# One order of pieces for the three later batches: rewriting the issue lists of five engines

## The chip, the cores and the metric

The kernel runs on one core of one Trainium2 chip. The metric is the device time of one execution in microseconds (us), less is better. The kernel before took 447.46 us (median of 3 runs, 446.96 to 448.86). One further execution was profiled; it took 444.95 us, and its span from the first to the last instruction is 443.1 us.

## What is computed

The input x holds four batches of 512 tokens with 512 features in fp32. One transformer layer is computed, cut here to what matters:

```
h  = layernorm(x)
q, kv = h @ W_q.T, h @ W_kv.T            # 16 heads of 32
q, kv = fft(q), fft(kv), each divided by its L2 norm over the head
kv = cumsum(kv, over the tokens)
x  = x + real(ifft(q * kv)) @ W_o.T      # the attention half
h  = layernorm(x)
g  = silu((h @ fp8(gate_w)) * gate_scale) * ((h @ fp8(up_w)) * up_scale)
x  = x + (g @ fp8(down_w)) * down_scale  # the feed-forward half, 1536 wide
```

## The kernel before

A batch b is worked in 4 row tiles t of 128 tokens; the feed-forward half runs in 12 steps i of 128 columns, numbered n = 12b + i over all batches. Each of the five engines (PE, ACT, DVE, POOL and the DMA queue SP) runs a list of pieces, strictly in the order in which it is written, and pieces of different engines meet on semaphores. Products that need more than one pass are split in a high part, made by ACT as a copy, and a low part, made by DVE or POOL as a difference.

For one row tile the attention half goes through these pieces. `pe_qk(b,t,w)` (L281): 12 matmuls, q for w=0 and kv for w=1. `act_qk` squares and copies the result, `dve_sum` sums the squares. After all 8 of them come `dve_norm_head`, `act_sqrt1`, `dve_norm_tail` and `dve_scale(b,t,w)` (L893), which divides by the norm. `act_ks` and `pool_ks(b,t)` (L238) make the two parts of the scaled kv. `pe_tri(b,t)` (L294), 2 matmuls, is the running sum over the 128 tokens of the tile. `act_row(b,t)` (L569) then copies the last row and sends it by a small DMA to row 0 of the next tile's position, where `pool_ks(b,t+1)` adds it (L1242) before `act_ks(b,t+1)` and `pool_ks` go on: this is the carry, and it makes the four `pe_tri` of a batch a chain. `dve_product(b,t)` (L899) and `pool_product(b,t)` (L1246, three operations, the last L1257) multiply q with the running sum. `pe_pT` (L307) transposes, `act_pT` and `dve_pT` take the two parts away, `pe_o` (L315) multiplies by W_o with 12 matmuls, and `dve_o` adds to x. After the four tiles come the second layernorm and `pe_hT` (L328), `act_hT`, `dve_hT`.

The feed-forward step n is `pe_gate_up` (L352): 8 matmuls into the one bank bg and 8 into the one bank bu; `act_silu(n)` empties bg, `dve_f(n)` empties bu, `act_fu(n)` and `dve_fu(n)` make the two parts in a buffer with two places, and `pe_down(n)` (L387) adds 8 matmuls to the four banks bd. `act_fu(n)` waits for `pe_down(n-2)`. All attention pieces after batch 0 share the two banks ba, taken in turn by the order that `tenancies()` gives; that order is the same before and after.

Batch 0's attention half, and beside batch 0's feed-forward half the attention half of batch 1, stand in a prologue that is written out piece by piece. It also folds the Fourier matrix into W_q and W_kv (`pe_fold`), into W_o (`pe_wo_high`, `pe_wo_low`), and rounds the gate, up and down weights to fp8 in 18 parts (`sp_weights`, `act_half`, `dve_round`). From then on a loop runs over b = 1, 2, 3: the feed-forward half of b beside the attention half of b + 1, which for b = 3 does not exist. In the kernel before the loop over b holds an inner loop over i with conditions such as `if 5 <= i <= 8: pe_pT(e, nxt, i - 5)`. In it `pe_down(n-1)` follows `pe_gate_up(n)`, with the attention pieces between or behind them.

Of the kernel before, what the change touches and what calls it, by code (L numbers as in the profile page):

```python
# [14 lines left out]
NB = 4  # L15
NT = 4
KT = 4
D = 512
NI = 12
# [63 lines left out]
def build(nc, x, xT, w_q, w_kv, woT, gate_w, up_w, down_w, gs_d, us_d, ds_d, cst_d, cst2_d, out):  # L83
    ctx = ExitStack()
    with ctx:
# [305 lines left out]
        def tensor_program(e):  # L391
# [12 lines left out]
            pe_wo_high(e, 0)  # L404
            pe_wo_high(e, 1)
            pe_wo_high(e, 2)
            pe_wo_low(e, 0)
            pe_pT(e, 0, 0)
            pe_wo_high(e, 3)
            pe_tri(e, 0, 1)  # L410
            pe_wo_low(e, 1)
            pe_wo_low(e, 2)
            pe_wo_low(e, 3)
            pe_tri(e, 0, 2)
            pe_o(e, 0, 0)
            pe_pT(e, 0, 1)
            pe_tri(e, 0, 3)
            pe_pT(e, 0, 2)
            pe_o(e, 0, 1)
            pe_o(e, 0, 2)  # L420
            pe_pT(e, 0, 3)
            pe_qk(e, 1, 0, 0)
            pe_o(e, 0, 3)
            pe_hT(e, 0, 0)
            pe_qk(e, 1, 0, 1)
# [3 lines left out]
            pe_hT(e, 0, 2)  # L429
            pe_hT(e, 0, 3)  # L430
            pe_qk(e, 1, 2, 0)
# [5 lines left out]
            pe_gate_up(e, 0, 2)  # L437
            pe_down(e, 0)
            pe_gate_up(e, 0, 3)
            pe_gate_up(e, 0, 4)  # L440
            pe_down(e, 1)
            pe_tri(e, 1, 0)
            pe_gate_up(e, 0, 5)
            pe_down(e, 2)
            pe_gate_up(e, 0, 6)
            pe_pT(e, 1, 0)
            pe_tri(e, 1, 1)
            pe_down(e, 3)
            pe_o(e, 1, 0)
            pe_gate_up(e, 0, 7)  # L450
            pe_pT(e, 1, 1)
            pe_down(e, 4)
            pe_tri(e, 1, 2)
            pe_down(e, 5)
            pe_o(e, 1, 1)
            pe_gate_up(e, 0, 8)
            pe_down(e, 6)
            pe_pT(e, 1, 2)
            pe_tri(e, 1, 3)
            pe_gate_up(e, 0, 9)  # L460
            pe_down(e, 7)
            pe_o(e, 1, 2)
            pe_pT(e, 1, 3)
            pe_gate_up(e, 0, 10)
            pe_o(e, 1, 3)
            pe_down(e, 8)
            pe_gate_up(e, 0, 11)
            pe_hT(e, 1, 0)
            pe_hT(e, 1, 1)
            pe_down(e, 9)  # L470
            pe_hT(e, 1, 2)
            pe_hT(e, 1, 3)
            pe_down(e, 10)
            for b in range(1, NB):
                for i in range(NI):
                    n, nxt = b * NI + i, b + 1
                    pe_gate_up(e, b, i)
                    if nxt < NB:
                        if i in (0, 1):
                            pe_qk(e, nxt, i, 0)  # L480
                            pe_qk(e, nxt, i, 1)
                        if i == 2:
                            pe_qk(e, nxt, 3, 0)
                            pe_qk(e, nxt, 3, 1)
                        if i == 4:
                            pe_tri(e, nxt, 0)
                        if 6 <= i <= 9:
                            pe_o(e, nxt, i - 6)
                        if 5 <= i <= 8:
                            pe_pT(e, nxt, i - 5)  # L490
                        if i == 10:
                            pe_hT(e, nxt, 0)
                            pe_hT(e, nxt, 1)
                        if i == 11:
                            pe_hT(e, nxt, 3)
                    if 0 < n < NB * NI - 2:
                        pe_down(e, n - 1)
                    if nxt < NB:
                        if i == 1:
                            pe_qk(e, nxt, 2, 0)  # L500
                            pe_qk(e, nxt, 2, 1)
                        if 5 <= i <= 7:
                            pe_tri(e, nxt, i - 4)
                        if i == 10:
                            pe_hT(e, nxt, 2)
# [140 lines left out]
        def scalar_program(e):  # L646

            act_center(e, 0)
            act_minus(e)
            act_center(e, 1)  # L650
            act_center(e, 2)
            act_center(e, 3)
# [3 lines left out]
            act_x(e, 0, 1)  # L656
            act_x(e, 0, 2)
            act_wf(e, 0, 2)
            act_x(e, 0, 3)
            act_wf(e, 0, 3)  # L660
            act_wf(e, 1, 0)
            act_wf(e, 1, 1)
# [5 lines left out]
            act_first_root(e)  # L668
            act_half(e, 2)
            act_qk(e, 0, 0, 1)  # L670
            act_triangle(e)
            act_qk(e, 0, 1, 0)
            act_qk(e, 0, 1, 1)
            act_sqrt1(e, 0, [0, 1])
            act_qk(e, 0, 2, 0)
            act_ks(e, 0, 0)
            act_qk(e, 0, 2, 1)
            act_qk(e, 0, 3, 0)
            act_ks(e, 0, 1)
            act_half(e, 3)  # L680
# [4 lines left out]
            act_x(e, 1, 1)  # L685
            act_wo_low(e, 0)
# [3 lines left out]
            act_ks(e, 0, 2)  # L690
            act_wo_low(e, 1)
            act_wo_low(e, 2)
            act_pT(e, 0, 0)
            act_ks(e, 0, 3)
            act_wo_low(e, 3)
            act_pT(e, 0, 1)
            act_pT(e, 0, 2)
            act_x(e, 1, 2)
            act_half(e, 4)
            act_x(e, 1, 3)  # L700
            act_pT(e, 0, 3)
            act_half(e, 5)
            act_half(e, 6)
            act_sqrt2(e, 0, [0, 1])
            act_hT(e, 0, 0)
            act_qk(e, 1, 0, 0)
            act_sqrt2(e, 0, [2, 3])
            act_hT(e, 0, 1)
            act_qk(e, 1, 0, 1)
            act_qk(e, 1, 1, 0)  # L710
            act_half(e, 7)
            act_hT(e, 0, 2)
            act_qk(e, 1, 1, 1)
            act_hT(e, 0, 3)
            act_qk(e, 1, 2, 0)
            act_qk(e, 1, 2, 1)
# [780 lines left out]
```

## Time and profile before

| | us |
|---|---|
| median of 3 runs | 447.46 (446.96 to 448.86) |
| profiled execution | 444.95 |
| its span | 443.1 |
| PE busy | 425.4, 96% of the span |
| DVE, ACT, POOL busy | 270.6, 186.3, 103.3 |

An engine's busy time is the sum of its instructions' durations in the profile. A row of the timeline gives the start of a run of like instructions, how long it lasts, and in brackets the idle time of the engine ahead of it with what ended it.

### The profile page before, as it was taken

How to read it: one execution, taken by the hardware profiler on the slowest of the kernel's cores; microseconds unless marked ns; L12 is line 12 of the kernel's file. 1: busy time of each engine (PE TensorE's matmuls, PEld its weight loads, DVE VectorE, ACT ScalarE, POOL GpSimd, SP SyncE). 2: the span in 40 equal slices, each digit the busy share in tenths (PEclk: the TensorE clock that was granted, in tenths of full speed). 3: DMA queues.
4: the chain of work that ended last, by engine and by line, in shares of the span. 5: the costliest groups of instructions: out<-in, count | busy, mean ns of one | idle time of the engine just before them, and what ended most of it. 6: DMA issues, size and time to landing. Idle time of an engine off the chain costs nothing.

```text
span 443.1 us, 5468 instructions
## 1 busy us (share of the span) xinstructions
PE 425.4 (96%) x1976; PEld 279.8 (63%) x1976; DVE 270.6 (61%) x488; ACT 186.3 (42%) x299; POOL 103.3 (23%) x107
## 2 busy tenths in 40 slices
PE   4999999999999999999799999999989999999995
PEld 4885678655666666875466657777456665555554
DVE  5999699989687773357655373445836463523224
ACT  4768345665524363236342352345333252222230
POOL 0404820001646002301537110400354100400002
PEclk9999999999999999999999999999999999999999
DMA  8980481011150000700000000320000000200002
GB/s 251 333 324 22 118 278 60 0 29 24 45 191 1 0 2 0 226 12 1 0 0 25 25 2 0 122 69 0 0 2 1 1 0 1 95 1 1 0 1 95
DMA packets 17595, 26.14 MB, mean 59 GB/s; under 512 B 1824, under 2 KB 8224, under 8 KB 17568
## 3 DMA queue, kind: packets, MB, share of 16 engines
q1 hardware_dynamic: 17280, 25.77, 17.5%
q8 instruction: 16, 0.26, 0.2%
q14 instruction: 11, 0.09, 0.1%
q10 hardware_dynamic: 288, 0.02, 0.0%
HBM read 21.57 MB, written 4.19 MB: 58 GB/s over the span
## 4 chain that ended last, share of the span: by engine, by line
PE 86%; POOL 5%; DMA 2%; DVE 2%; ACT 2%; issue 1%; SPq 0%; DVEq 0%; POOLq 0%
PE bd L383 18%; PE bg L367 18%; PE bu L367 18%; PE ba L290 15%; PE ba L324 7%; PE bd L290 3%; POOL qk L1253 2%; PE ba L333 1%; DMA gu<-gate_w_dram 1%; PE ba L303 1%; DMA hT<-w_q_dram 1%; POOL ks L1244 1%; PE ba L312 1%; PE bd L276 1%; POOL qk L1254 1%
## 5 line engine op out<-in xcount | busy, mean ns | idle before, releaser
L383 PE MATMUL bd<-dw,fu 128*128 128x512 f32 x376 | 99.3, 405 | 0.0
L367 PE MATMUL bg<-hT,gu 128*128 128x512 f16 x384 | 91.1, 380 | 0.0
L367 PE MATMUL bu<-hT,gu 128*128 128x512 f16 x384 | 90.7, 379 | 0.0
L383 PEld LDWEIGHTS bd<-dw,fu 128*128 128x128 f32 x376 | 69.6, 188 | 15.7
L972 DVE SCALAR_TENSOR_TENSOR ff<-bu,us,sl 128x512 f32<-128x512 f32 x48 | 35.9, 749 | 62.6 <-PE bu L367 60.8
L290 PE MATMUL ba<-wf,xTs 128*128 128x512 f32 x288 | 69.2, 396 | 0.0
L367 PEld LDWEIGHTS bu<-hT,gu 128*128 128x128 f16 x384 | 37.6, 98 | 45.3
L367 PEld LDWEIGHTS bg<-hT,gu 128*128 128x128 f16 x384 | 34.8, 98 | 45.6 <-issue 8.2
L290 PEld LDWEIGHTS ba<-wf,xTs 128*128 128x128 f32 x288 | 53.7, 188 | 12.0 <-POOL xTs L1236 0.2
L607 ACT ACTIVATE sl<-bg,gs 128x512 f32<-128x512 f32 x48 | 33.0, 688 | 60.8 <-PE bg L367 60.0
L1244 POOL TENSOR_TENSOR ks<-qk,ks 128x512 f16<-128x512 f32 x16 | 19.0, 1185 | 127.1 <-ACT ks L567 127.1
L617 ACT ACTIVATE fu<-ff 128x512 fp32r<-128x512 f32 x47 | 29.5, 629 | 36.2 <-DVE ff L972 33.2
L1262 POOL TENSOR_TENSOR h<-ff,h 128x512 f32<-128x512 f32 x14 | 17.5, 1283 | 114.4 <-DVE ff L994 114.4
L851 DVE TENSOR_REDUCE S<-tu 128x16 f32<-128x512 f32 x32 | 21.7, 682 | 33.4 <-ACT tu L538 33.4
L977 DVE TENSOR_TENSOR fu<-ff,fu 128x512 fp32r<-128x512 f32 x47 | 34.2, 728 | 12.8 <-ACT fu L617 12.8
L324 PE MATMUL ba<-wo,pT 128*128 128x512 f32 x144 | 36.6, 403 | 0.0
L538 ACT ACTIVATE tu<-ba 128x512 f32<-128x512 f32 x24 | 14.3, 597 | 47.4 <-PE ba L290 47.4
L324 PEld LDWEIGHTS ba<-wo,pT 128*128 128x128 f32 x144 | 27.1, 188 | 6.5
L1253 POOL TENSOR_TENSOR qk<-tu 128x256 f32<-128x256 f32 x14 | 16.2, 1160 | 40.2 <-DVE tu L919 40.2
L1236 POOL TENSOR_TENSOR xTs<-xTr,xTs 128x512 fp32r<-128x512 f32 x12 | 15.8, 1322 | 34.4 <-ACT xTs L524 34.4
L567 ACT ACTIVATE ks<-qk 128x512 f16<-128x512 f32 x16 | 10.1, 633 | 30.4 <-POOL qk L1242 23.5
L896 DVE TENSOR_TENSOR qk<-qk,sc 128x512 f32<-128x512 f32 x32 | 21.9, 724 | 0.1
(161 smaller groups left out, 465.3 us busy)
## 6 DMA issues: line engine op xcount, KB each, us to landing
h<-x_dram SPq DMA_DIRECT2D x16, 256.0 KB, 4.1
out_dram<-h SPq DMA_DIRECT2D x16, 256.0 KB, 2.0
xTr<-xT_dram SPq DMA_DIRECT2D x12, 256.0 KB, 4.5
hT<-w_q_dram SPq DMA_DIRECT2D x4, 256.0 KB, 3.2
gu<-w_kv_dram SPq DMA_DIRECT2D x4, 256.0 KB, 5.6
h<-xT_dram SPq DMA_DIRECT2D x4, 256.0 KB, 6.4
hT<-up_w_dram SPq DMA_DIRECT2D x2, 512.0 KB, 4.7
hT<-gate_w_dram SPq DMA_DIRECT2D x2, 512.0 KB, 6.9
```

The lines of the kernel that those rows point to most:

```text
L290: m = e.matmul(ba[i][:, :], xTs[:, part_x, k, P * t:P * t + P], wf[:, w, part_w, k, :], start=k == 0 and part_x == part_w, stop=k == KT - ...
L324: m = e.matmul(ba[i][:, :], src[:, part_p, P * j:P * j + P], wo[:, part_w, j, :], start=j == 0 and part_p == part_w, stop=j == KT - 1 and ...
L367: m = e.matmul(bk[:, :], gu[:, c, 4 * w + k, col:col + P], hT[:, b % 2, part, k, :], start=k == 0 and part == 0, stop=k == KT - 1 and part ...
L383: m = e.matmul(bd[t][:, :], fu_at(n)[:, part, P * t:P * t + P], dw[:, i, :], start=i == 0 and part == 0, stop=i == NI - 1 and part == 1)
L607: e.activation(sl[:, n % 2, :], bg[:, :], ACT.Silu, scale=gs[:, i:i + 1]).then_inc(a_silu, 1)
L617: e.activation(fu_at(n)[:, 0, :], ff[:, n % 2, :], ACT.Copy).then_inc(a_fu, 1)
L851: e.tensor_reduce(S[:, t, NH * w:NH * w + NH], v, AX.X, ALU.add).then_inc(v_sum, 1)
L896: e.tensor_tensor(split_heads(qk[:, t, w, :]), split_heads(qk[:, t, w, :]), head_scale(t, w), ALU.mult).then_inc(v_kn if w else v_qn, 1)
L972: e.scalar_tensor_tensor(out=ff[:, n % 2, :], in0=bu[:, :], scalar=us[:, i:i + 1], in1=sl[:, n % 2, :], op0=ALU.mult, op1=ALU.mult).then_i ...
L977: e.tensor_tensor(fu_at(n)[:, 1, :], ff[:, n % 2, :], fu_at(n)[:, 0, :].bitcast(F32), ALU.subtract).then_inc(v_fu, 1)
L1244: e.tensor_tensor(ks[:, 1, t, :], qk[:, t, 1, :], ks[:, 0, t, :], ALU.subtract).then_inc(p_ks, 1)
L1253: e.tensor_tensor(q_re, t_re, t_im, ALU.subtract).then_inc(p_re, 1)
```

## The change

All five issue lists get a new order; no function that computes, no buffer and no semaphore is changed, and every piece is issued as often as before. The inner loop over i is gone: for each b the pieces stand in one list. PE's list for the loop:

```diff
             for b in range(1, NB):
-                for i in range(NI):
...
-                    pe_gate_up(e, b, i)
...
+                nxt = b + 1
+                if nxt < NB:
+                    pe_qk(e, nxt, 0, 0)
+                    pe_qk(e, nxt, 0, 1)
+                pe_gate_up(e, b, 0)
+                pe_down(e, b * NI - 1)
...
+                pe_gate_up(e, b, 3)
+                pe_down(e, b * NI + 1)
+                pe_gate_up(e, b, 4)
+                pe_down(e, b * NI + 2)
+                if nxt < NB:
+                    pe_tri(e, nxt, 0)
+                pe_gate_up(e, b, 5)
+                pe_down(e, b * NI + 3)
+                pe_gate_up(e, b, 6)
+                if nxt < NB:
+                    pe_pT(e, nxt, 0)
+                    pe_tri(e, nxt, 1)
+                pe_down(e, b * NI + 4)
+                if nxt < NB:
+                    pe_o(e, nxt, 0)
+                pe_gate_up(e, b, 7)
+                if nxt < NB:
+                    pe_pT(e, nxt, 1)
+                pe_down(e, b * NI + 5)
+                if nxt < NB:
+                    pe_tri(e, nxt, 2)
+                    pe_o(e, nxt, 1)
+                pe_gate_up(e, b, 8)
+                if nxt < NB:
+                    pe_pT(e, nxt, 2)
+                pe_gate_up(e, b, 9)
+                if nxt < NB:
+                    pe_tri(e, nxt, 3)
+                    pe_o(e, nxt, 2)
+                pe_down(e, b * NI + 6)
+                if nxt < NB:
+                    pe_pT(e, nxt, 3)
+                pe_down(e, b * NI + 7)
+                if nxt < NB:
+                    pe_o(e, nxt, 3)
+                pe_down(e, b * NI + 8)
+                pe_gate_up(e, b, 10)
+                if nxt < NB:
+                    pe_hT(e, nxt, 0)
+                    pe_hT(e, nxt, 1)
+                pe_gate_up(e, b, 11)
...
```

In POOL's loop `pool_ks(nxt, 0)` and `pool_ks(nxt, 1)` now both stand ahead of `pool_product(nxt, 0)`, where before the product stood between them. In DVE's loop only `dve_scale` of (0,1), (0,0), (1,0), (1,1), (2,0) stand ahead of `dve_product(nxt, 0)`, and behind it `dve_f`, `dve_fu`, `dve_pT(0)` and `dve_product(1)`; before, three `dve_scale` came close behind the first product.

The prologue is reordered as well. The parts that are spoken of below:

```diff
 SP
+            sp_weights(e, 3)
+            sp_weights(e, 8)
             sp_x(e, 0, 2)
+            sp_x(e, 1, 0)
+            sp_weights(e, 11)
+            sp_weights(e, 9)
+            sp_scales(e)
+            sp_wo(e)
...
 ACT
             act_center(e, 2)
+            act_first_root(e)
             act_center(e, 3)
...
 PE
             pe_wo_high(e, 0)
+            pe_tri(e, 0, 1)
+            pe_pT(e, 0, 0)
             pe_wo_high(e, 1)
+            pe_wo_low(e, 0)
...
+            pe_pT(e, 0, 1)
+            pe_o(e, 0, 0)
             pe_tri(e, 0, 2)
             pe_tri(e, 0, 3)
```

Before, `sp_wo` stood ahead of `sp_x(e, 1, 0)`, which waits for `dve_round(2)`; `act_first_root`, the first square root, stood behind `act_half(1)`; and `pe_tri(0, 1)` came behind `pe_wo_high(3)`, `pe_o(0, 0)` behind `pe_tri(0, 2)`.

## Rows read from the trace of the kernel before

**Rows 1.** The page, busy time and the 40 slices of 11.08 us:

```profile
PE 425.4 (96%) x1976; PEld 279.8 (63%) x1976; DVE 270.6 (61%) x488; ACT 186.3 (42%) x299; POOL 103.3 (23%) x107
...
GB/s 251 333 324 22 118 278 60 0 29 24 45 191 1 0 2 0 226 12 1 0 0 25 25 2 0 122 69 0 0 2 1 1 0 1 95 1 1 0 1 95
```

**Rows 2.** Busy time in stretches: attention 0, prologue's rest, b = 1, 2, 3:

```profile
15.32:64.56 49.24, 47.21 (x211) 35.05 (x210) 42.04 (x87) 29.89 (x54) 19.29 (x22) 1.00 0.60 200
64.56:163.51 98.95, 98.89 (x468) 64.55 (x466) 82.84 (x138) 52.48 (x79) 20.68 (x21) 1.00 0.14 46
163.51:268.14 104.63, 102.32 (x473) 66.85 (x473) 56.56 (x103) 41.69 (x68) 30.24 (x29) 1.00 0.10 31
268.14:372.37 104.23, 101.99 (x473) 66.95 (x472) 54.82 (x102) 37.94 (x61) 22.18 (x23) 1.00 0.06 21
372.37:431.90 59.53, 59.53 (x271) 32.86 (x271) 18.75 (x27) 15.22 (x23) 4.98 (x4) 1.00 0.05 19
```

**Rows 3.** PE's waits: us in total, times, longest:

```profile
PE ba L312 <- POOL qk L1257: 3.2, 2, 1.6
PE bd L303 <- POOL ks L1244: 1.3, 1, 1.3
```

**Rows 4.** Timeline of PE in b = 1, steps 4 to 9:

```profile
201.20 1.90 PE L367 MATMUL bg<-hT,gu 128*128 128x512 f16 x8
...
206.50 1.90 PE L367 MATMUL bg<-hT,gu 128*128 128x512 f16 x8
...
209.97 0.59 PE L303 MATMUL ba<-ks,tr 128*128 128x512 f16 x2
...
217.44 0.63 PE L312 MATMUL ba<-cst,qk 128*128 128x128 f32 x4 [1.58 <-POOL qk L1257]
...
220.56 0.59 PE L303 MATMUL ba<-ks,tr 128*128 128x512 f16 x2 [0.65 <-POOL ks L1244]
...
238.69 0.59 PE L303 MATMUL ba<-ks,tr 128*128 128x512 f16 x2
```

**Rows 5.** Timeline of ACT, DVE and POOL in b = 1:

```profile
211.22 0.52 ACTq L575 DMA_DIRECT2D qk<-qk  x1
...
213.16 0.68 DVE L977 TENSOR_TENSOR fu<-ff,fu 128x512 fp32r<-128x512 f32 x1
213.32 2.92 POOL L1253 TENSOR_TENSOR qk<-tu 128x256 f32<-128x256 f32 x1 [4.96 <-DVE tu L919]
213.77 1.88 DVE L896 TENSOR_TENSOR qk<-qk,sc 128x512 f32<-128x512 f32 x3
...
217.24 1.26 POOL L1242 TENSOR_TENSOR qk<-qk 1x512 f32<-1x512 f32 x1
219.25 1.16 POOL L1244 TENSOR_TENSOR ks<-qk,ks 128x512 f16<-128x512 f32 x1 [0.74 <-ACT ks L567]
...
240.75 0.73 POOL L1253 TENSOR_TENSOR qk<-tu 128x256 f32<-128x256 f32 x1 [2.20 <-DVE tu L919]
```

**Rows 6.** DMA issues: KB each, median us from issue to landing:

```profile
gu<-woT_dram SPq DMA_DIRECT2D x1, 1024.0 KB, 10.9
...
qk<-qk ACTq DMA_DIRECT2D x9, 2.0 KB, 1.6
```

**Rows 7.** Timeline of SP and PE in the prologue:

```profile
22.18 0.67 SPq L1367 DMA_DIRECT2D gu<-woT_dram  x1
27.88 0.34 SPq L1332 DMA_DIRECT2D h<-x_dram  x1
...
37.81 1.88 PE L342 MATMUL ba<-gu,sl 128*128 128x512 f32 x4
```

**Rows 8.** Timeline of ACT at the start of the prologue:

```profile
10.06 0.73 ACT L518 ACTIVATE hT<-hT,wmv 128x512 f32<-128x512 f32 x1 [0.43 <-DVE wmv L827]
...
22.34 1.28 ACT L628 ACT_TABLE_LOAD   x1
23.64 0.20 ACT L628 ACTIVATE Q<-Q 128x1 f32<-128x1 f32 x1
```

More of the change, by code:

```diff
@@ new lines, in scalar_program @@
+                act_fu(e, b * NI + 1)
+                if nxt < NB:
+                    act_qk(e, nxt, 3, 0)
+                act_fu(e, b * NI + 2)
+                act_silu(e, b * NI + 3)
+                if nxt < NB:
+                    act_qk(e, nxt, 3, 1)
+                    act_sqrt1(e, nxt, range(NT))
+                act_silu(e, b * NI + 4)
+                if nxt < NB:
+                    act_ks(e, nxt, 0)
+                    act_row(e, nxt, 0)
+                act_fu(e, b * NI + 3)
@@ new lines, in scalar_program @@
+                if b + 2 < NB:
+                    act_x(e, b + 2, 0)
+                act_silu(e, b * NI + 5)
+                if nxt < NB:
+                    act_ks(e, nxt, 1)
+                act_fu(e, b * NI + 4)
+                act_fu(e, b * NI + 5)
+                act_silu(e, b * NI + 6)
+                if nxt < NB:
+                    act_pT(e, nxt, 0)
+                    act_row(e, nxt, 1)
+                act_fu(e, b * NI + 6)
+                if b + 2 < NB:
+                    act_x(e, b + 2, 1)
@@ new lines, in scalar_program @@
+                act_silu(e, b * NI + 7)
+                if nxt < NB:
+                    act_ks(e, nxt, 2)
+                    act_pT(e, nxt, 1)
+                    act_row(e, nxt, 2)
+                act_silu(e, b * NI + 8)
+                if nxt < NB:
+                    act_ks(e, nxt, 3)
+                    act_pT(e, nxt, 2)
+                act_fu(e, b * NI + 7)
+                act_fu(e, b * NI + 8)
+                if nxt < NB:
+                    act_pT(e, nxt, 3)
+                act_silu(e, b * NI + 9)
@@ new lines, in scalar_program @@
+                if nxt < NB:
+                    act_sqrt2(e, nxt, range(NT))
+                act_fu(e, b * NI + 9)
+                if b + 2 < NB:
+                    act_x(e, b + 2, 2)
+                act_silu(e, b * NI + 10)
+                act_fu(e, b * NI + 10)
+                if nxt < NB:
+                    act_hT(e, nxt, 0)
+                    act_hT(e, nxt, 1)
+                act_silu(e, b * NI + 11)
+                if nxt < NB:
+                    act_hT(e, nxt, 2)
+                act_fu(e, b * NI + 11)
@@ new lines, in vector_program @@
+                dve_f(e, b * NI + 3)
+                if nxt < NB:
+                    dve_norm_tail(e, nxt, range(NT))
+                    dve_scale(e, nxt, 0, 1)
+                    dve_scale(e, nxt, 0, 0)
+                dve_f(e, b * NI + 4)
+                if nxt < NB:
+                    dve_scale(e, nxt, 1, 0)
+                    dve_scale(e, nxt, 1, 1)
+                    dve_scale(e, nxt, 2, 0)
+                dve_fu(e, b * NI + 3)
+                if nxt < NB:
+                    dve_product(e, nxt, 0)
```

678 lines of the change are left out of this document (337 added, 341 removed).

## The prediction

> **What bounds the kernel now.** I read the page first. PE is busy for 425.4 of 443.1 us [rows 1], and the change neither adds nor takes away one of its instructions, so all that can be won is time in which PE stands idle: 17.7 us at most. The table of stretches says where that is [rows 2]: subtract PE's busy time from each length. Attention 0 has 2.0 us, the rest of the prologue 0.1, the loop's b = 1 and b = 2 have 2.3 and 2.2, and b = 3 none. The remaining 11 us are the start, ahead of the first projections, and the end, where the last output leaves; the lists order the end as before. The granted clock is 1.00 in every stretch, the upper of TensorE's two levels (2.4 GHz), and PE idles too little anywhere for it to be in question.
>
> Then PE's waits, which name the causes [rows 3]: in total 3.2 us of the first transposes of b = 1 and 2, pT(nxt,0), for the last operation of POOL's product, and 1.3 us in attention 0 for POOL's part of ks. The timeline of b = 1 shows the two gaps of a loop [rows 4]: 1.58 us ahead of pT(2,0) and 0.65 ahead of tri(2,1). b = 2 repeats them within 0.01 us. The other engines' rows tell why [rows 5]: the product of tile 0 started on POOL at 213.32, its first operation took 2.92 us where the same operation at 240.75 took 0.73, while DVE ran operations with two inputs from SBUF beside it (a `dve_fu` at 213.16, three `dve_scale` at 213.77). Only behind it did POOL add the carry (217.24) and make ks of tile 1 (219.25), for which tri(2,1) waited.
>
> **The loop, tile 0.** Prices of pieces on PE: a gate pair is 209.97 - 206.50 = 3.47 us, gate pair and down together 206.50 - 201.20 = 5.30, so a down is 1.83 [rows 4]. Before, one down and one gate pair lay between the tri and the pT of tile 0, and PE came to pT 217.44 - 1.58 - 209.97 = 5.9 us after the tri began, while the product was ready after 7.5. After the change a gate pair, a down and a gate pair lie there, with the tri itself (about 0.4) 9.2 us. What must happen in that time is more than before, since POOL now makes ks of tile 1 first. Counted from the tri's start: the row is sent at 1.25 (211.22) and lands 1.6 later, 2.85 [rows 5, 6]; from the carry's start to ks's start are 219.25 - 217.24 = 2.0, and ks takes 1.16, so 6.0; the product takes 0.73 twice and some 0.3, near 1.8, so 7.8 [rows 5]. One `dve_fu` (0.68) may hold POOL up in it: 8.5. That leaves 0.7 us. With the 2.2 us by which a product was lengthened before (2.92 less 0.73), it would be 10.0 and PE would wait 0.8. But no row of scales is issued beside it now, only f, fu, pT and the next product, so I take 8.5. The tri of tile 1, directly behind this pT, needs ks, which is ready at 6.0 to 6.7. Both gaps go: 2.23 us in each of two loops, -4.5.
>
> **The loop, the other tiles.** Between tri and pT of tiles 1 and 2 lie 8.1 us (down, o, gate pair) and 6.3 (o, gate pair); an o piece is 12 matmuls against a down's 8, so some 2.75. Before, a gate pair and an o lay there and nothing waited. At tile 3 only an o and a down are left, with the tri 5.0 us. In the trace POOL's product starts 240.75 - 238.69 = 2.1 after the tri's start and takes near 1.8, which is 3.9: it fits by 1.1. pT(3) to o(3) is one down and the transpose, 2.2 us, and in it lie ACT's copy and DVE's difference behind the two of fu(8): four operations of 0.63 to 0.7 that overlap pairwise, about 2.0. The three downs 6, 7, 8 stand together; fu(8) waits for the first, then needs 219.25 - (217.24 + 1.26) = 0.75 for a copy and its signal on ACT [rows 5] and 0.68 on DVE, 1.4 against the 1.83 of down(7). These two places are thin, so I add +0.3 for both loops and keep 0 to +1.0. What is behind the waiting `act_fu(8)` on ACT is `act_pT(3)` and `act_silu(9)`, the next gate pair is two downs away, so nothing else is late. For b = 3 the attention pieces are missing, the same fit holds, and its 59.53 us were all busy before: 0.
>
> **The loop's seam.** qk(nxt,0,0) now comes ahead of gate pair 0, directly behind down(10). Its last k block needs `pool_x(3)`, which ACT's list puts behind `act_hT(3)`, the piece that PE released 1.8 us before. Two ACT copies (0.7 each with their signal) and POOL's 1.3 make 2.7; PE needs it after down (1.83) and 9 matmuls (three quarters of an o's price, 2.0), at 3.8. Hidden by 1.1, nothing in the sum; without the cover it would cost 2.7 less 1.8, once.
>
> **The prologue.** Attention 0 can win its 2.0 us of idle and lose by two new orders. First, `sp_wo` now stands behind `sp_x(1,0)`, which waits for round(2) and was issued at 27.88, where wo had gone out at 22.18 [rows 7]. By my count of DVE's new order round(2) ends some 0.6 earlier, so x goes out at 27.3; ahead of wo are then x (0.25 MB), two weight parts (0.5 each) and the scales (0.26), with wo 2.5 MB. At the 333 GB/s of the fullest slice [rows 1] that is 7.6 us, with 2 us from issue to first data the landing is near 37; PE wants wo at 37.81 [rows 7]. The other bound is wo's own 10.9 us [rows 6] from its issue, near 30.1: 41.0, and PE waits 3.2. Since the queue is empty at 27.3, I take the first, with +0.4. Second, pT(0,1) is now ahead of o(0,0), and its product on POOL lies beside DVE's norm tail and scales, which lengthened a product by 2.2 above. I give this back about half of what is gained by tri(0,1) coming earlier. Sum for attention 0: -1.3 of the 2.0, +0.4, +0.6: -0.3, bounds -2.0 and +3.0. For the rest of the prologue DVE is busy 82.84 of 98.95 us [rows 2], but PE idles 0.06 there; walking through the new order I find each round done before its gate pair (the nearest, round(16), by some 0.4 us). 0, up to +0.6.
>
> **The start.** The first root brings its table load, 1.28 us, from 22.34 to between the center pieces 2 and 3 [rows 8]. DVE's new order releases center(2) some 0.8 earlier, and center(3) waited 0.43 for DVE anyway, so most of it lies in that hole: +0.15, bounds 0 and +1.3. The fold's last quarter waits for it.
>
> The Trainium skill, page ScalarE: Activation LUTs, section What ACT_TABLE_LOAD costs, gives a switch 1283 ns for the load and 1380 ns more for a drain. The row agrees with the first and shows nothing of the second, since the square root starts at 23.64, 0.02 us behind the load's end; by the page the start would cost 1.5 us instead of 0.15, and the sum below would be -3.0.
>
> **Sum.** -4.46 + 0.3 - 0.3 + 0 + 0.15 = -4.3 us. The profiled execution took 444.95, 1.85 more than its span, so the changed one should take 440.6. The median of the runs is 2.5 above the profiled one; with the same distance I predict 447.46 - 4.3 = 443.1 us. No change is within 0.5%, 2.2 us, which is about what a measurement here can tell.
>
> **Rivals.**
> 1. The prologue wins too: all 2.0 us of attention 0 go, and of the hidden waits inside busy stretches some more. 447.46 - 4.5 - 2.0 = 441.0, down to 440. For it: producers stand earlier in every list. Against: DVE is busy 42.04 of 49.24 us there [rows 2]. Chance 0.2.
> 2. The stall only moves: POOL's first product is lengthened as before, PE waits 0.8 at pT(0) and up to 0.5 at each of the thin places. Each loop wins only 1 us, the kernel 2.0: 445.4. For it: the 2.92 us row. Against: no scales beside it. Chance 0.13.
> 3. The drain at a table load is real in the new place: 447.46 - 3.0 = 444.5. Against it the row of 23.64. Chance 0.03.
> 4. wo lands late: at 41.0 PE waits 3.2, ACT's square root and so the norm tail stand behind `act_wo_high(0)`, and 447.46 - 4.3 + 2.8 = 446.0 is within the noise. Chance 0.09.
> 5. Slower, by the same mechanism further on: from a landing at 44.5, 6.5 us behind PE's need, the loops' gain is gone and 2.2 more. It decides if round(2) or the weights ahead of wo come 3.5 us later than in my upper bound. 447.46 - 4.3 + 6.5 = 449.7. Chance 0.06.
>
> My forecast has 0.49. Its own range is 441.6 to 444.6. Over all cases 440.3 to 446.3 leaves out the slower case and the ends of the others, less than 2 in 10. Faster: forecast, rivals 1 and 3 and about a third of rival 2, 0.76. Same: 0.17. Slower: 0.07.
>
> **What would show it.** In the changed profile PE's list of waits should have no entry for L1257 or L1244 over 0.5 us in b = 1 and 2, and the stretches of b = 1 and 2 should be near 102.3 us each. POOL's first product operation of tile 0 should take 0.7 to 1.5 us, and PE should come to pT(0) 9.2 us after the tri. The matmul of wo_high(0) should start at 38 to 39; a gap there with woT as its releaser is rival 4 or 5. The fold should end at most 0.3 us later. The prediction is wrong if PE idles in b = 1 for over 1.5 us, or if attention 0 ends later than in the kernel before by over 1 us.

## The result

The changed kernel takes 439.88 us (median of 6 runs, 439.43 to 440.89) against 446.69 us for the kernel before (6 runs, 446.2 to 448.86). The ratio is 0.9844, 95% interval 0.982 to 0.9867: 1.6% faster. I had forecast 443.1 us with a range of 440.3 to 446.3, so the direction was right and the time lies 0.4 us below the range. The change itself was larger than forecast: 6.8 us against 4.3.

The profiled execution took 439.65 us, its span is 437.8 us. Against the profiled execution of before (444.95 and 443.1) that is 5.3 us less, where the sum of the prediction had 4.3. The page of the changed kernel, its busy times and its slices:

```profile
PE 425.1 (97%) x1976; PEld 280.2 (64%) x1976; DVE 276.2 (63%) x488; ACT 185.2 (42%) x299; POOL 104.9 (24%) x107
...
GB/s 215 328 293 117 141 304 4 0 49 2 72 155 15 1 2 0 85 156 0 2 0 2 49 1 1 47 146 0 0 2 1 1 0 1 96 1 1 0 0 97
```

PE's busy time is the same as in [rows 1] within 0.3 us, so what was won is idle time and, for a small part, the spacing between matmuls. A row of the stretches gives the window, its length, the busy time of PE, PEld, DVE, ACT and POOL with their numbers of instructions, the granted clock and the DMA share. The stretches that answer to [rows 2] (the start, attention 0, the prologue's rest, b = 1, b = 2, b = 3):

```profile
0.00:15.96 15.96, 9.41 (x64) 8.92 (x65) 10.35 (x29) 9.86 (x16) 3.58 (x7) 1.00 0.80 264
15.96:64.26 48.30, 47.22 (x208) 34.67 (x206) 43.33 (x88) 27.79 (x52) 19.70 (x22) 1.00 0.70 222
64.26:163.54 99.28, 99.28 (x470) 65.00 (x469) 85.46 (x137) 54.71 (x82) 23.77 (x23) 1.00 0.11 36
163.54:265.38 101.84, 101.84 (x473) 67.14 (x472) 57.48 (x102) 39.83 (x65) 26.69 (x27) 1.00 0.11 32
265.38:367.21 101.83, 101.83 (x473) 66.93 (x472) 56.26 (x101) 37.74 (x61) 23.62 (x24) 1.00 0.07 21
367.21:426.50 59.29, 59.29 (x271) 32.87 (x270) 17.93 (x26) 14.66 (x23) 4.98 (x4) 1.00 0.05 18
```

Each stretch ends with the first matmul of the next; attention 0 is cut here at hT(0,0), in [rows 2] one transpose later. The loop starts at 163.54, before at 163.51: the whole prologue gave nothing. Loops b = 1 and b = 2 together took 372.38 - 163.51 = 208.87 us, to the first matmul of b = 3, and now take 367.21 - 163.54 = 203.67: 5.2 less. PE is never idle in them. Its waits in the whole changed kernel:

```profile
PE ba L276 <- ACT hT L556: 6.6, 3, 5.4
PE bd L312 <- POOL qk L1371: 0.4, 1, 0.4
PE bg L324 <- ACT wo L682: 0.4, 1, 0.4
PE bu L349 <- ACT wo L678: 0.2, 1, 0.2
```

The first line is the start, the other three are attention 0. The two lines of [rows 3] are gone, and so is the line of the loops' second gap, which the kernel before had:

```profile
PE ba L303 <- POOL ks L1244: 1.3, 2, 0.7
```

The timeline of PE in b = 1, from the tri of tile 0 to its transpose, shows why (compare [rows 4]):

```profile
210.03 0.61 PE L303 MATMUL ba<-ks,tr 128*128 128x512 f16 x2
210.47 1.89 PE L367 MATMUL bg<-hT,gu 128*128 128x512 f16 x8
212.20 1.89 PE L367 MATMUL bu<-hT,gu 128*128 128x512 f16 x8
213.74 2.18 PE L383 MATMUL bd<-dw,fu 128*128 128x512 f32 x8
215.76 1.90 PE L367 MATMUL bg<-hT,gu 128*128 128x512 f16 x8
217.49 1.89 PE L367 MATMUL bu<-hT,gu 128*128 128x512 f16 x8
219.22 0.60 PE L312 MATMUL ba<-cst,qk 128*128 128x128 f32 x4
219.66 0.59 PE L303 MATMUL ba<-ks,tr 128*128 128x512 f16 x2
```

And POOL's timeline beside it, which answers to [rows 5]:

```profile
213.32 1.27 POOL L1356 TENSOR_TENSOR qk<-qk 1x512 f32<-1x512 f32 x1 [3.71 <-DMA qk<-qk]
215.34 1.16 POOL L1358 TENSOR_TENSOR ks<-qk,ks 128x512 f16<-128x512 f32 x1 [0.74 <-ACT ks L605]
216.47 1.18 POOL L1367 TENSOR_TENSOR qk<-tu 128x256 f32<-128x256 f32 x1
217.60 0.73 POOL L1368 TENSOR_TENSOR qk<-tu 128x256 f32<-128x256 f32 x1
218.46 0.24 POOL L1371 COPY qk<-tu 128x32 f32<-128x32 f32 x1
```

PE comes to pT(0) 219.22 - 210.03 = 9.19 us after the tri and finds the product, which ended at 218.70, 8.67 after the tri. The margin is 0.5 us. The prediction had 9.2 and 8.5. The product's first operation took 1.18 us in place of 2.92. POOL's part of ks of tile 1 was ready 216.50 - 210.03 = 6.5 us after the tri, where the prediction had 6.0 to 6.7.

### The profile page after: what moved, and what is told of

Its sections match the earlier page's. It is cut to its first block, busy times and chain, and to the rows that moved or that the text cites. A ratio compares the mean times of both kernels' runs of the same rounds, so it can differ in the third digit from the quotient of the medians.

```text
span 437.8 us, 5468 instructions
## 1 busy us (share of the span) xinstructions
PE 425.1 (97%) x1976; PEld 280.2 (64%) x1976; DVE 276.2 (63%) x488; ACT 185.2 (42%) x299; POOL 104.9 (24%) x107
## 4 chain that ended last, share of the span: by engine, by line
PE 93%; DMA 2%; POOL 2%; ACT 1%; DVE 1%; issue 0%; SPq 0%; DVEq 0%; POOLq 0%
PE bd L383 20%; PE bg L367 19%; PE bu L367 19%; PE ba L290 15%; PE ba L324 8%; PE bd L290 3%; PE ba L333 1%; PE bd L324 1%; PE ba L303 1%; PE ba L312 1%; DMA hT<-w_q_dram 1%; DMA xTr<-xT_dram 1%; PE bd L276 1%; PE bu L290 1%; PE bg L290 1%; POOL xTs L1350 1%
## 5 line engine op out<-in xcount | busy, mean ns | idle before, releaser
L367 PEld LDWEIGHTS bu<-hT,gu 128*128 128x128 f16 x384 | 37.6, 98 | 45.3
L1051 DVE TENSOR_TENSOR fu<-ff,fu 128x512 fp32r<-128x512 f32 x47 | 37.5, 802 | 22.8 <-ACT fu L655 22.6
L970 DVE TENSOR_TENSOR qk<-qk,sc 128x512 f32<-128x512 f32 x32 | 22.8, 744 | 0.2
L1367 POOL TENSOR_TENSOR qk<-tu 128x256 f32<-128x256 f32 x14 | 13.5, 967 | 33.6 <-DVE tu L993 33.6
L929 DVE BATCH_NORM_STATS2 bst<-h 128x6 f32<-128x512 f32 x16 | 10.9, 682 | 9.4 <-DMA h<-x_dram 9.4
```

Of the source, the lines that this page charges most:

```text
L367: m = e.matmul(bk[:, :], gu[:, c, 4 * w + k, col:col + P], hT[:, b % 2, part, k, :], start=k == 0 and part == 0, stop=k == KT - 1 and part ...
L970: e.tensor_tensor(split_heads(qk[:, t, w, :]), split_heads(qk[:, t, w, :]), head_scale(t, w), ALU.mult).then_inc(v_kn if w else v_qn, 1)
L1051: e.tensor_tensor(fu_at(n)[:, 1, :], ff[:, n % 2, :], fu_at(n)[:, 0, :].bitcast(F32), ALU.subtract).then_inc(v_fu, 1)
```

## The experiments

No kernel here changes what is computed: each only puts the same pieces in another order. Times are medians; the ratio is to the kernel before, run on the same chip in the same comparison. The later comparisons were four; in three of them the kernel before stood a second time as a kernel of its own, and in three the changed one did. Where it did not (the second), a version can only be set against the kernel before.

**Which half of the change carries the gain.** The loops alone: the prologue lists of before with the new loops. One line of PE's list, against the kernel before, stands for the whole:

```diff
             for b in range(1, NB):
-                for i in range(NI):
-                    pe_gate_up(e, b, i)
...
+                pe_gate_up(e, b, 6)
+                if nxt < NB:
+                    pe_pT(e, nxt, 0)
+                    pe_tri(e, nxt, 1)
```

> The five prologues of the kernel before, with the new loops. Theory (the whole gain is the loops'): the two profiles reach the loop at 163.5 us both, so this should be as fast as the changed kernel, 0.984 to 0.988 of the kernel before, and PE's stretches of b = 1 and b = 2 should be 102.3 us each. Rival (the new prologue gives over 1 us that the one profile of before hides): 0.989 or more, 442 us or above.

Measured: 442.58 us against 444.05, ratio 0.9965 (0.9951 to 0.9978). That is less than the loops' whole gain. PE's waits and a row of windows at the start of b = 1 tell why:

```profile
PE ba L290 <- POOL xTs L1347: 1.7, 2, 1.4
PE bd L303 <- POOL ks L1355: 1.1, 1, 1.1
```

```profile
160.00:166.00 6.00, 4.67 (x25) 3.49 (x23) 3.40 (x6) 2.81 (x5) 1.19 (x1) 1.00 0.01 3
166.00:168.00 2.00, 1.60 (x5) 1.06 (x6) 0.00 (x0) 0.00 (x0) 1.31 (x2) 0.92 0.00 0
168.00:170.00 2.00, 2.00 (x6) 1.52 (x6) 0.00 (x0) 0.00 (x0) 0.00 (x0) 0.50 0.00 0
170.00:172.00 2.00, 2.00 (x8) 1.60 (x7) 0.00 (x0) 0.00 (x0) 0.00 (x0) 0.73 0.00 0
172.00:174.00 2.00, 2.00 (x10) 0.89 (x9) 0.00 (x0) 0.00 (x0) 0.00 (x0) 1.00 0.00 0
```

The new loop begins with qk(2,0), and the old prologue leaves `act_x(2,2)` and `act_x(2,3)` to its very end: PE waits 1.45 and 0.27 us for the last x. Behind that wait the granted clock is at its lower level (0.50, 1.2 GHz) for some 3 us. What the four last windows lack of a clock of 1.00, times their 2 us, is 1.7 us. In this execution the projection took 172.49 - 163.15 = 9.3 us, in the changed kernel 168.99 - 163.54 = 5.45; the two waits and the clock are 3.4 of the 3.9 us between them. None of that is in the loops proper, where no wait is left. So the seam that the prediction took as covered is a real need of the loop's new order, met in the changed kernel by its new prologue. By its number the rival would be right (442 us or above), but its reason, a gain of the new prologue by itself, falls with the next two versions. The first of them moves only those two ACT pieces:

```diff
 ACT, prologue
             act_fu(e, 8)
+            act_x(e, 2, 2)
             act_silu(e, 9)
...
             act_fu(e, 10)
+            act_x(e, 2, 3)
...
             act_fu(e, 11)
-            act_x(e, 2, 2)
-            act_x(e, 2, 3)
```

> The prologues of the kernel before with the new loops, and ACT's two copies of x for batch 2 (tiles 2 and 3) moved from the end of its prologue to behind act_fu(8) and act_fu(10), where the first projection of the new loop finds them done. Theory (the loops carry the gain, and the first version of this kernel lost 1.7 us at the seam for want of x): the two waits for POOL's xTs at the loop's start are gone and the time is 1.5 us below loop_only, within 0.7 us of the changed kernel. Rival (the new prologue is worth over 1 us by itself): no better than 441.5 when before is at 444.

Measured: 440.36 us against 444.29, ratio 0.9903 (0.9887 to 0.9919). The changed kernel in the same comparison:

> The changed kernel, unchanged, on another chip than the first time. Theory (the kernel before takes 444 to 447 us depending on the chip and on how its POOL and DVE operations fall, the changed one has no such wait left and stays at 439.5 to 440.3): on a chip where before takes about 444 the ratio is near 0.991, a gain of 4.0 us. Rival (the first ratio, 0.984, holds everywhere): 437.5 or less there.

Measured: 440.41 us, ratio 0.9908 (0.9888 to 0.9927). The loops with the two x pieces give all of the gain, as far as the two intervals can tell.

**The other half.** The new prologue with the loops of before:

```diff
             for b in range(1, NB):
-                pe_gate_up(e, b, 6)
-                if nxt < NB:
-                    pe_pT(e, nxt, 0)
-                    pe_tri(e, nxt, 1)
...
+                for i in range(NI):
+                    pe_gate_up(e, b, i)
```

> The five new prologues with the loops of the kernel before. Theory: 0.998 to 1.002 of the kernel before, and PE's two gaps of a loop (1.6 us at the transpose of tile 0, 0.65 at the running sum of tile 1) are there again in b = 1 and b = 2. Rival (the prologue carries over 1 us): 0.997 or less.

Measured: 444.44 us against 444.05, ratio 1.0006 (0.9995 to 1.0017). The gaps of [rows 4] are back: 0.49 and 1.11 us in b = 1, 1.57 and 0.65 in b = 2. The new prologue alone is worth nothing.

**How steady are the two kernels?** The kernel before, run again as it is:

> The kernel before, unchanged, profiled once more. The first profile of before took 444.95 us, less than each of its six timed runs (446.2 to 448.86), while the changed kernel's profile (439.65) lies among its own (439.43 to 440.89). Theory (a chance low in one profile): this one takes 446 to 447 us, and its rows show where some 1.5 us lie that the first profile lacks. Rival (a profiled execution of this kernel is always that much faster): about 445 again.

Measured: 443.87 against 444.05, ratio 0.9996 (0.9985 to 1.0007). Its POOL and DVE in b = 1 are not those of [rows 5]:

```profile
212.72 1.11 POOL L1253 TENSOR_TENSOR qk<-tu 128x256 f32<-128x256 f32 x1 [4.96 <-DVE tu L919]
213.79 1.17 POOL L1254 TENSOR_TENSOR qk<-tu 128x256 f32<-128x256 f32 x1
215.10 0.51 POOL L1257 COPY qk<-tu 128x32 f32<-128x32 f32 x1
215.57 1.72 POOL L1242 TENSOR_TENSOR qk<-qk 1x512 f32<-1x512 f32 x1
```

```profile
213.17 2.99 DVE L896 TENSOR_TENSOR qk<-qk,sc 128x512 f32<-128x512 f32 x3
```

The same work on the same two engines, and here they take turns: the three scales take 2.99 us and POOL's operations 1.11 and 1.17, where in [rows 5] the scales took 1.88 and POOL's first operation 2.92. PE then waits 0.49 and 1.10 us per loop in place of 1.58 and 0.65. In the third profile of the kernel before (fourth row of the table below) b = 1 shows the one form and b = 2 the other. A third and a fourth execution of before and of the changed kernel:

> The kernel before, profiled a third time. It has shown two patterns of gaps in a loop, 1.58 + 0.65 and 0.49 + 1.10 us, whose first part hangs on whether POOL's first product operation is held up for the whole of DVE's three scales (2.92 us) or takes turns with them (1.11 us). Theory (turns between POOL and DVE fall differently from run to run and chip to chip, and only this kernel feels them): one of the two patterns again, or a third, with PE's gaps of a loop between 1.5 and 2.3 us, and the kernel at 444 to 447. Rival: the gaps are as in the second profile and the difference of the chips lies elsewhere.

> The changed kernel, unchanged, beside the version with two edits. Theory: from the first projection to the end its span is 421.8 us within 0.3, as in its two profiles so far (437.8 - 15.96 and 438.3 - 16.37), whatever the chip; 439.5 to 440.5 in all. Rival (it varies as the kernel before does, by 2 us and more).

> The kernel before, profiled a fourth time. Open is why it took 446.7 us in the first comparison and 444.0 to 444.6 in the three others. Theory (TensorE's clock falls for some 3 us behind a PE gap in some executions, which costs 1.6 us each, and on one chip more often): if it takes 446 or more here, the profile shows a stretch behind pT(nxt,0) at the lower clock; if it takes 444 to 445, it shows none. Rival (another stretch, such as attention 0, is longer on that chip): 446 or more with all stretches at the full clock.

> The changed kernel, unchanged, on the same chip as the fourth profile of before. Theory: 439.5 to 440.5 whatever before takes, since it has no PE gap over 0.5 us behind the fold. Rival (chips differ as a whole): it moves with before, 442 or more if before is at 446.7.

| comparison | before | before as a kernel of its own | changed | ratio of changed (95%) | gaps per loop of before |
|---|---|---|---|---|---|
| first | 446.69 | | 439.88 | 0.9844 (0.982 to 0.9867) | 1.58 + 0.65 |
| second | 444.05 | 443.87 | | | 0.49 + 1.10 |
| third | 444.29 | | 440.41 | 0.9908 (0.9888 to 0.9927) | |
| fourth | 444.61 | 444.64 | 440.03 | 0.989 (0.9871 to 0.9909) | 0.49 + 1.12, then 1.57 + 0.66 |
| fifth | 443.92 | 444.09 | 439.13 | 0.9893 (0.9877 to 0.991) | 0.50 + 1.12, 0.49 + 1.12 |

All 107 later runs of the kernel before lie between 443.15 and 446.07, median 444.14; the 15 later runs of the changed one have a median of 440.03. Their difference is 4.1 us. The changed kernel is where it was in the first comparison, the kernel before is 2.5 us lower.

The profiles show how steady the work itself is once the start is left out. From the first projection (at 15.96, 16.37, 15.63 and 15.70 us) to the end of the span the changed kernel took 421.8, 421.9, 421.8 and 421.6 us. The kernel before took 427.8, 425.4, 426.8 and 425.7, from first projections at 15.32, 15.77, 16.14 and 15.65. The first of these four, on which the prediction rests, is the longest.

**Is it the scales that no longer lie beside the product?** The three `dve_scale` put back directly behind product 0:

```diff
 DVE
                     dve_product(e, nxt, 0)
+                    dve_scale(e, nxt, 2, 1)
+                    dve_scale(e, nxt, 3, 1)
+                    dve_scale(e, nxt, 3, 0)
...
                     dve_product(e, nxt, 1)
-                    dve_scale(e, nxt, 2, 1)
...
-                    dve_scale(e, nxt, 3, 1)
-                    dve_scale(e, nxt, 3, 0)
```

> The changed kernel with three dve_scale pieces of each loop issued directly behind the product of tile 0, as before the change. Theory (DVE operations with two inputs from SBUF hold POOL up; that was the 2.92 us operation): POOL's ks of tile 1 and its product come 1 to 1.9 us later, PE waits 0.5 to 1.4 us at the first transpose of b = 1 and b = 2, and the kernel takes 1 to 3 us more. Rival (the distance on PE covers it anyway): same time within 0.3 us.

Measured: 441.08 us, ratio 0.9924 (0.9907 to 0.9942), 0.7 us behind the changed kernel of the same comparison. The wait is not where I looked for it:

```profile
218.29 1.90 PE L367 MATMUL bu<-hT,gu 128*128 128x512 f16 x8 [0.35 <-DVE ff L1046]
220.02 0.60 PE L312 MATMUL ba<-cst,qk 128*128 128x128 f32 x4
```

The scales took 2.85 us from 214.72, and POOL's ks took 1.60 us beside them in place of 1.16. The product still ended at 219.49, 0.5 us ahead of pT(0). What came late was `dve_f`, which stands behind the scales and empties bu: 0.35 us in each loop. So neither half of the expectation holds as it stands: the distance on PE covers POOL's product, and the place of the scales is worth 0.35 us a loop by way of `dve_f`.

**Is it POOL's new order?** POOL's product 0 put back ahead of ks of tile 1:

```diff
 POOL
                     pool_ks(e, nxt, 0)
-                    pool_ks(e, nxt, 1)
                     pool_product(e, nxt, 0)
+                    pool_ks(e, nxt, 1)
```

> The changed kernel with POOL's product of tile 0 back ahead of its ks of tile 1. Theory (the longer way between tri(0) and pT(0) on PE is what counts, the order on POOL is free): no PE wait over 0.3 us in b = 1 and 2, same time within 0.5 us. Rival (ks must come first, since the chain of carries is the longer one): PE waits at tri(1), and the kernel takes over 1 us more.

Measured: 439.6 us, ratio 0.9893 (0.9878 to 0.9909). That is 0.8 us below the changed kernel of the same comparison, with intervals that overlap (0.9888 to 0.9927), and there is no wait in the loops. With 9.2 us on PE, POOL's order is free.

**The distance itself.** pT(0) ahead of gate pair 6, one gate pair less between tri and pT:

```diff
 PE
-                pe_gate_up(e, b, 6)
                 if nxt < NB:
                     pe_pT(e, nxt, 0)
+                pe_gate_up(e, b, 6)
+                if nxt < NB:
                     pe_tri(e, nxt, 1)
```

> The changed kernel with pT(nxt,0) ahead of gate pair 6 instead of behind it, so that one gate pair and two downs... of the way between tri(0) and pT(0) one gate pair is gone: 5.7 us instead of 9.2. Theory (the product is ready 8.4 to 8.7 us after the tri begins, POOL doing ks of tile 1 first): PE waits 2.7 to 3.0 us at the transpose in b = 1 and in b = 2, and the kernel takes 5.4 to 6 us more than the changed one, more than it gained. Rival (the gain came from other things, the product is ready at 6 us): under 1 us a loop.

Measured: 449.1 us against 444.61, ratio 1.0103 (1.0078 to 1.0127), 9.1 us above the changed kernel of the same comparison. PE in b = 2:

```profile
318.13 2.18 PE L383 MATMUL bd<-dw,fu 128*128 128x512 f32 x8
323.04 0.93 PE L312 MATMUL ba<-cst,qk 128*128 128x128 f32 x4 [2.73 <-POOL qk L1372]
323.76 3.32 PE L367 MATMUL bg<-hT,gu 128*128 128x512 f16 x8
326.92 1.89 PE L367 MATMUL bu<-hT,gu 128*128 128x512 f16 x8
```

```profile
323.00:324.00 1.00, 0.96 (x5) 0.84 (x6) 0.00 (x0) 0.00 (x0) 0.00 (x0) 0.61 0.00 0
324.00:325.00 1.00, 1.00 (x3) 0.30 (x2) 0.00 (x0) 0.00 (x0) 0.00 (x0) 0.50 0.08 16
325.00:326.00 1.00, 1.00 (x4) 0.41 (x3) 0.00 (x0) 0.00 (x0) 0.00 (x0) 0.50 0.00 0
326.00:327.00 1.00, 1.00 (x5) 0.38 (x4) 0.00 (x0) 0.00 (x0) 0.00 (x0) 0.68 0.00 0
```

In the profiled pair the spans differ by 446.2 - 437.4 = 8.8 us. Two waits, 2.80 and 2.73 us, are 5.5 of them; the product ended 8.5 us after the tri (218.19 - 209.65), as expected. Behind the second the clock was at its lower level for some 3 us: from the transposes' start to the bu group's it took 326.92 - 323.04 = 3.88 us. In b = 1 of the same run, at the upper level, the same pieces took 2.19 (0.46 for the transposes, 1.73 for the group), so the lower clock cost 1.7. Behind the first, of the same length, it stayed at 1.00 (216 to 226 us). In the three runs that were not profiled the mean granted clock was 0.989 to 0.990, in the profiled one 0.992, and they took 0.9 to 1.7 us longer; whether there it fell behind both waits no trace shows. Of the other 1.6 us, 1.2 came after the start of the last down group (12.1 us from there to the end of the span against 10.9 in the changed kernel of this comparison). All of this lies behind the issue of the first output transfer, which stands 5.7 us after that group in both; why the output took longer is not shown. The last 0.4 us is not traced to a cause. With the product ahead of ks on POOL as well:

> As pt_early, with POOL's product of tile 0 back ahead of its ks of tile 1. Theory (the product is then ready 6.2 to 6.6 us after the tri begins, PE comes after 5.7): PE waits 0.5 to 1.0 us a loop and its clock stays up, so the kernel takes 1 to 2.5 us more than the changed one, where pt_early took 9 more. Rival (what pt_early lost beside its two waits has nothing to do with their length): 3 us or more above the two waits again.

Measured: 440.81 us against 443.92, ratio 0.9931 (0.9916 to 0.9946), 1.7 above the changed kernel. The two kernels differ by one exchange on POOL and, each taken against the changed kernel of its own comparison, by 9.1 - 1.7 = 7.4 us. The wait is 0.64 us in each loop:

```profile
216.28 0.63 PE L312 MATMUL ba<-cst,qk 128*128 128x128 f32 x4 [0.64 <-POOL qk L1372]
```

The clock was 1.00 from 200 to 340 us there, behind both waits. So with one gate pair less it matters that POOL makes the product first, and with 9.2 us it does not.

**The start.** The first square root put back behind `act_half(1)`:

```diff
 ACT, prologue
             act_center(e, 2)
-            act_first_root(e)
             act_center(e, 3)
...
             act_half(e, 1)
+            act_first_root(e)
```

> The changed kernel with the first square root, and its table load, back behind the second weight part. Theory: center(3) starts 0.6 us earlier, the fold's gap of 0.97 us shrinks to about 0.3, and the kernel takes 0.5 to 0.65 us less than the changed one, if no later producer sets attention 0's end. Rival (attention 0 is bound by another chain, DVE's or the xTs of POOL): the gain at the fold is given back by the first output of attention 0, and the time is that of the changed kernel within 0.2.

Measured: 439.61 us against 444.05, ratio 0.9902 (0.9886 to 0.9918): beside the changed kernel's ratios of 0.989 to 0.9908 in the other comparisons nothing is to be seen; it did not run in this one. The load takes 1.28 us in either place. ACT's timeline of the changed kernel:

```profile
9.31 1.28 ACT L666 ACT_TABLE_LOAD   x1
10.61 0.20 ACT L666 ACTIVATE Q<-Q 128x1 f32<-128x1 f32 x1
```

The kernel with the root put back:

```profile
22.05 1.28 ACT L666 ACT_TABLE_LOAD   x1
23.35 0.20 ACT L666 ACTIVATE Q<-Q 128x1 f32<-128x1 f32 x1
```

Center(3) started at 10.23 us here and at 10.71 in the changed kernel. PE's gap of 0.97 us ahead of the fold's last quarter, in which the changed kernel waits for it, is gone. Still the first projection came at 16.83, not before 15.96, since PE's small matmuls ran at half rate for longer (see the last section). So neither the gain nor the rival's reason is shown.

**An attempt at a better kernel.** The same, and `act_x(1,1)` moved behind `act_wo_low(3)`, so that the two small waits for wo would go:

```diff
 ACT, prologue
             act_sqrt1(e, 0, [2, 3])
-            act_x(e, 1, 1)
...
             act_wo_low(e, 3)
+            act_x(e, 1, 1)
```

> The changed kernel with the first square root back behind the second weight part and ACT's copy of x(1,1) moved from ahead of act_pT(0,0) to behind act_wo_low(3). Theory: the 0.22 and 0.42 us waits of PE for ACT's parts of W_o go, so that from the first projection to the end it takes 421.2 to 421.4; with 0.5 less at the fold it is 0.6 to 1.1 us faster than the changed kernel. Rival (attention 0 is bound by product 3 on POOL, the 0.43 us wait takes over what is won): within 0.3 us of the changed kernel.

Measured: 441.02 us against 444.61, ratio 0.9912 (0.9887 to 0.9938). The attempt failed: the waits for wo stay at 0.23 and 0.42, and pT(0,3) now waits 1.77 us, where the changed kernel has 0.44. This execution runs 0.98 us behind that of the changed kernel (wo_high(0) at 39.43 against 38.45). `act_x(1,1)` at 46.52 now stands ahead of `act_ks(0,2)`, POOL's ks and its halves of x(1,1) and x(1,2) came some 0.3 us later by this measure, and so did the load of x(1,3), which waits for the first of them (issued at 51.38 against 50.09). Then `act_x(1,3)` (55.31 against 54.01), POOL's half of it (56.02 against 54.73) and product 3 follow. The other 1.0 us is the product's own: its second operation took 1.25 us and its copy 1.05, in the changed kernel 0.74 and 0.58, with a rounding piece of DVE beside them in both (58.66, 1.63 us, and 58.06, 1.23 us). No version beats the changed kernel by more than its interval.

## Where the prediction was right, and the step that failed

**The loops, gaps: right.** The term was -4.46 for four gaps, and in the profiled pair these four went. The experiments bear out the reason: the distance on PE (one gate pair less brings 2.8 us of wait), and that the loops, with the two x pieces made in time, bring the whole gain. As a size the term was the high end: it took one profiled execution for the kernel, and other executions of before show 1.6 us per loop in place of 2.23, so 3.2 to 4.5 for both.

**The loops, thin places: wrong, +0.3 not needed.** pT(3) to o(3) has no wait (245.99 to 248.35), and the three downs in a row of b = 3 run as 24 matmuls in 5.83 us. What I left out was a gain of the other sign: 5.2 less 4.47 leaves 0.73 us without any wait named. It is spacing, or waits too small to be listed. Less its waits, b = 1 took 104.63 - 2.23 = 102.40 us before and 101.84 now, b = 2 104.23 - 2.24 = 101.99 and 101.83. So 0.56 of it lies in b = 1 and 0.16 in b = 2. One part comes in both loops: from the start of the bu group to pT(0) PE took 1.89 us before, the wait already left out, and takes 1.73 now. Another is a place where b = 1 of the kernel before was slower than its b = 2 though the list is the same: from down to tri(3) 2.16 against 1.94 us. The rest is not shown. It is not that f16 and fp32 groups change places less often: they do so 24 times in a loop before and 28 times now.

**The seam: right, and needed.** Nothing waits there in the changed kernel. Without the cover the profiled execution of the loops alone shows its price: 1.7 us of wait and 1.7 at the lower clock. My 0.9 was too low for the wait and had no such clock in it; "PE idles too little anywhere for it to be in question" holds for the changed kernel only.

**The prologue: right as a sum, by other parts.** My terms were +0.15 for the start, -0.3 for attention 0 and 0 for the rest, -0.15 together; measured, with the cut at the first gate matmul (82.38 us before, 82.52 after), are +0.64, (82.52 - 15.96) - (82.38 - 15.32) = -0.50 and (163.54 - 82.52) - (163.51 - 82.38) = -0.11, together +0.03. PE's idle time in attention 0 is 1.08 us in place of 2.03, and none of the 1.08 is a loss that I had priced. It is 0.22 and 0.42 us for ACT's parts of W_o and 0.44 us ahead of pT(0,3), at 58.27, for product 3. The product beside DVE's norm tail did not come late: its two operations took 0.73 us each (42.07 and 42.76), and pT(0,1) at 44.76 waited for nothing. `sp_wo` was issued at 29.53 and landed 8.1 us later, at 37.6, where I had 37 from the queue's rate; wo_high(0) started at 38.45 without a wait, 22.49 us after the first projection, in both kernels (37.81 - 15.32). So the +0.4 for wo was not needed either.

```profile
29.53 0.43 SPq L1487 DMA_DIRECT2D gu<-woT_dram  x1
```

```profile
gu<-woT_dram SPq DMA_DIRECT2D x1, 1024.0 KB, 8.1
```

So rivals 4 and 5 did not come: the 10.9 us of [rows 6] was the time of a queue with more ahead of it (2.5 MB issued in the 4.7 us before it, against 1.5 MB in 2.9 us now). Rival 1 named the time nearest to the measured one, 440 to 441, for a cause that did not come: the new prologue alone is worth nothing (1.0006). Rival 2 did not come: the product's first operation took 1.18 us. Nor did it in the run with pT early (1.17), whose waits of 2.8 us come from the shorter distance and not from a lengthened product. Rival 3 fell: with the load at 9.31 the root starts 0.02 us behind its end, as in [rows 8]. The Trainium skill, page ScalarE: Activation LUTs, section What ACT_TABLE_LOAD costs, has a further 1380 ns of drain; no run here shows it.

**The start: +0.15 against +0.64.** The first projection came at 15.96, before at 15.32. That is more than the 0.3 us that I had named as a bound for the fold's end, and PE waits 0.97 us there for the center piece behind the load. But the mean of the four profiles each is 15.92 against 15.72, 0.2 apart, and each kernel spreads over 0.7 to 0.8 us; with the root put back it was 16.83. The +0.15 fits this and is not shown by it.

**The step that failed: "with the same distance".** The profiled time was 440.6 by the sum and 439.65 measured, 0.95 too high, from the terms above. Then I added the 2.5 us by which the median of before stood above its profiled execution. For the changed kernel that distance is 0.2, and in the three later repeats of before it is 0.6, -0.1 and 0.7. The other 2.3 us of the miss are this step. Without it the sum gives 440.6 + 0.2 = 440.8 us, inside the stated range; with it the time lies outside. The profiled 444.95 was an ordinary value of the kernel before (the later median is 444.14); it was the three timed runs that stood high. Why the first comparison's runs of before are above all 107 later ones, while the changed kernel's are not higher than later, stays open; of the kernel before there is one trace from that time, and neither clock nor span of the timed runs is on record. Three causes are possible and none is shown. One is a clock that falls behind PE's gaps: the changed kernel has none in its loops, and such falls were seen behind gaps of 1.7 and 2.7 us, but no profile of the kernel before shows one behind its gaps of 1.6. A second is a less lucky mix of what the profiles show: the first one is the longest from the first projection on (427.8 us, with the long gap in both loops) and has the earliest start; behind a start of 16.4 us the same work would give 446.0 by my estimate, which reaches the lower runs and not 448.86. The third is the chip: the later comparisons ran on chips 3, 2, 2 and 13, the first chip is not on record. Measured against the kernel before as it ran in three of the later comparisons, the change is worth 3.9 to 4.8 us, which is about the predicted 4.3. In part this agreement is luck: in the three later profiles of before the gaps are worth 3.2 to 3.8 us and not 4.46, the thin places cost nothing and not 0.3, and the 0.7 us of spacing was not in the sum.

## What to carry to other kernels

In a hand-written issue order, count for each producer how long its whole chain takes from the piece that releases it (carry, copy, difference, product), at the worst turn of the engines that share it, and put that much of the bound engine's own work between; 0.5 us of margin was enough here, and POOL's order then no longer mattered; the place of DVE's scales still cost 0.35 us a loop, by way of another piece behind them. Check the seam: a loop whose first piece needs something early must find it made by the code ahead of the loop. And take the distance between a profiled execution and the timed runs for noise of one draw, not for a constant to add.

## What the runs showed of the hardware

**Clock.** In kernels with PE busy 96 and 97% of the time, a single wait was followed by some 3 us at the lower level of the clock (1.2 GHz): behind 1.45 + 0.27 us in the run of the loops alone and behind 2.73 us with pT early, costing 1.7 us each. It did not come behind a wait of 2.80 us in that same run, nor behind the 1.58 us of before, whose stretch reads 1.00 [rows 2]. So a short wait cost twice its length in one case (1.7 us and 1.7 more), and not every wait did.

**Two engines in turns.** DVE and POOL operations with two inputs from SBUF, beside each other, came out in one of two ways, from execution to execution and, in the third profile of before, from loop to loop of one execution: POOL stood still until DVE was done (2.92 us for an operation of 0.73, DVE's three scales 1.88), or they took turns (1.11 and 1.17 against 2.99). In both executions DVE's `dve_fu` had started about 0.15 us ahead of POOL's operation (213.16 against 213.32, and 212.57 against 212.72), so the order of issue was the same and the outcome was not. The Trainium skill, page SBUF — State Buffer, section Who interferes with whom, says that a DVE instruction with two SBUF inputs contends with a POOL instruction that reads SBUF, and that the order of issue decides who blocks; the rows agree with the first, and the second does not tell these two executions apart.

**The first matmuls.** PE's small matmuls of 128 columns at the start ran at half rate for some microseconds while the granted clock already read 1.00. Windows of the kernel with the root put back:

```profile
9.00:13.00 4.00, 4.00 (x21) 4.00 (x21) 4.00 (x12) 2.39 (x5) 1.28 (x1) 1.00 1.00 370
13.00:17.00 4.00, 4.00 (x36) 4.00 (x36) 3.79 (x8) 3.21 (x8) 2.80 (x2) 1.00 0.58 203
```

The first holds 21 matmuls, the second 36, with PE busy all through both. In the changed kernel's profile the faster pace was reached at about 9 us, here at about 13. The 16 matmuls from 9.98 to 13.34 took 3.36 us here; at the faster pace, 32 in 3.49 us, they would have taken 1.7. By this estimate the pace moves the start by up to 1.6 us, more than the whole table load of 1.28, though part of it fills time in which PE would otherwise wait for ACT (0.97 us in the changed kernel).
